# Two hidden layers of a decoder's FFN by seven block products over pairs of token groups

## The reference

```python
x = _layernorm(x + _L0_attn_ref(x, ...))           # a scan over 128 positions, 8 heads
x = _layernorm(x + _L0_xattn_ref(x, ctx, itok, proj_in, proj_out))   # 8 experts, all of them dense
x = _layernorm(x + _L0_ffn_ref(x, ...))

# the FFN: w1, w2 [1024, 256], h1, h2 [1024, 1024], w3 [256, 1024], all ternary (times 8), s: a scale per output
h = silu(x @ w1.T * w1_s) * (x @ w2.T * w2_s)
h = gelu(h @ h1.T * h1_s)
h = gelu(h @ h2.T * h2_s)
return h @ w3.T * w3_s
```

## Time and profile before

| | us |
|---|---|
| median of three runs (784.78 to 785.19) | 784.87 |
| span of the profiled execution, first to last instruction | 783.9 |
| TensorE busy in it | 775.0 (99%) |
| VectorE busy | 485.2 (62%) |
| ScalarE busy | 358.2 (46%) |
| GpSimd busy | 197.4 (25%) |

### The profile page before, as it was taken

The page is one execution under the profiler, slowest core; times in us unless marked ns, Lnnn a source line. Parts: engine busy times, 40 slices in busy tenths (PEclk is TensorE's granted clock), DMA queues, the critical chain, the costliest instruction groups (busy, mean ns, idle before and its releaser), DMA issues.

```text
span 783.9 us, 12001 instructions
## 1 busy us (share of the span) xinstructions
PE 775.0 (99%) x3827; PEld 654.8 (84%) x3827; DVE 485.2 (62%) x1146; ACT 358.2 (46%) x691; POOL 197.4 (25%) x233
## 2 busy tenths in 40 slices
PE   8999999999999999999999999999999999999996
PEld 6788888888888888888888888888888888888886
DVE  4789889876786878788665654327432654255113
ACT  6778743334433434343433364434443354335332
POOL 2776333325342525243342310000000000000001
PEclk9999999999999999999999999999999999999998
DMA  7800000002212231212211000100010001000000
GB/s 258 293 1 1 1 1 1 1 28 82 71 51 95 54 108 41 94 54 80 67 53 42 7 2 1 27 1 27 0 27 0 27 0 27 0 28 1 0 1 29
DMA packets 22414, 32.96 MB, mean 42 GB/s; under 512 B 8161, under 2 KB 12897, under 8 KB 22113
## 3 DMA queue, kind: packets, MB, share of 16 engines
q1 hardware_dynamic: 22080, 32.14, 13.4%
q10 hardware_dynamic: 288, 0.26, 0.1%
HBM read 28.72 MB, written 2.10 MB: 39 GB/s over the span
## 4 chain that ended last, share of the span: by engine, by line
PE 98%; DMA 1%; issue 0%; POOL 0%; ACT 0%; SPq 0%; DVE 0%; POOLq 0%
PE bank L1178 30%; PE bank L1071 15%; PE bank L927 10%; PE bank L955 8%; PE bank L1049 7%; PE bank L1050 7%; PE bank L1054 7%; PE bank L1070 6%; PE bank L1193 4%; PE bank L1074 2%; DMA wp_lo_f<-in_wproj 1%; PE bank L995 0%; PE bank L1027 0%; PE bank L1026 0%; POOL rstd L568 0%
## 5 line engine op out<-in xcount | busy, mean ns | idle before, releaser
L1071 PE MATMUL bank<-wx_both,hx_hi 128*128 128x512 f32 x512 | 191.5, 397 | 0.0
L798 ACT ACTIVATE hx_hi<-bank 128x512 fp32r<-128x512 f32 x128 | 76.4, 597 | 204.9 <-PE bank L1054 203.7
L573 POOL TENSOR_TENSOR x_tok<-right,x_tok 128x256 f32<-128x256 f32 x128 | 95.9, 750 | 210.9 <-ACT right L805 210.9
L1433 DVE SCALAR_TENSOR_TENSOR hx_lo<-bank,hx_hi 128x512 fp32r<-128x512 f32 x128 | 88.2, 689 | 70.9 <-ACT hx_hi L798 69.8
L1071 PEld LDWEIGHTS bank<-wx_both,hx_hi 128*128 128x128 f32 x512 | 96.2, 188 | 16.6
L1070 PE MATMUL bank<-wx_both,hx_lo 128*128 128x256 f32 x384 | 108.8, 283 | 0.0
L1178 PE MATMUL bank<-ha_hi_r,wf_hi_r 128*128 128x512 f32 x256 | 100.1, 391 | 0.0
L1551 DVE TENSOR_TENSOR ha_lo<-hf,ha_hi_r 128x512 fp32r<-128x512 f32 x64 | 44.1, 688 | 90.4 <-ACT hf L892 89.9
L1178 PE MATMUL bank<-ha_lo,wf_hi_r 128*128 128x512 f32 x256 | 99.8, 390 | 0.0
L1178 PE MATMUL bank<-hb_lo,wf_hi_r 128*128 128x512 f32 x256 | 99.7, 390 | 0.0
L1178 PE MATMUL bank<-hb_hi_r,wf_hi_r 128*128 128x512 f32 x256 | 99.7, 389 | 0.0
(11 more groups left out here) (192 smaller groups left out, 1446.9 us busy)
## 6 DMA issues: line engine op xcount, KB each, us to landing
stage<-in_wffn SPq DMA_DIRECT2D x44, 256.0 KB, 2.7
wx_raw<-in_wx SPq DMA_DIRECT2D x16, 512.0 KB, 4.0
x_tok<-in_x SPq DMA_DIRECT2D x1, 2048.0 KB, 12.9
out<-x_tok SPq DMA_DIRECT2D x16, 128.0 KB, 1.8
xs_lo_f<-in_xT SPq DMA_DIRECT2D x3, 512.0 KB, 6.3
wp_lo_f<-in_wproj SPq DMA_DIRECT2D x2, 512.0 KB, 7.3
ctx_sb<-in_ctx SPq DMA_DIRECT2D x1, 1024.0 KB, 6.6
itok_sb<-in_itok SPq DMA_DIRECT2D x1, 1024.0 KB, 8.6
```

Of the source, the lines that this page charges most:

```text
L573: pool.tensor_tensor(row, right[:, j % 2], row, ALU.add).then_inc(s_row_ok, 1)
L798: act.activation(hx_hi[:, place, c], bank[b][:, :], ACT.Relu).then_inc(s_relu_ok, 1)
L1071: mm = pe.matmul(DBANK[j][:, :].rearrange("p (h d) -> p h d", h=2), hx_hi[:, place, c, a], wo_hl[:, :, c], start=(c == 0), stop=(c == XC - 1))
L1433: dve.scalar_tensor_tensor(out=hx_lo[:, place, c], in0=bank[b][:, :], scalar=0.0, in1=hx_hi[:, place, c].bitcast(F32), op0=ALU.max, op1=AL ...
```

## The change

H1 and H2 are computed for two groups at once. The 1024 x 1024 weight is cut into 2 x 2 blocks of 512 x 512 and the activations of a pair of groups into 2 x 2 blocks of 512 features x 512 tokens (f11, f21 of the first group, f12, f22 of the second). Eight block products become seven by a form of Strassen's scheme: three sums of activation blocks per layer (t1 = f12 - f11, t2 = f22 - t1, t4 = f21 - t2 on VectorE; t3 = f22 - f12 on POOL, in place), four sums of weight blocks, and additions of the results (ScalarE copies a bank out, `snap`; VectorE adds the other bank, `block_11`, `block_22`, `block_12`). The gelu then runs once, on the finished block (`curved`). A product is four outputs m x four k x two parts, 32 matmuls.

The weights' block sums are made beside experts 2 to 5: SyncE loads a quad (four blocks of 128 x 512), POOL makes four sums (`block_sum`), ScalarE rounds the seven blocks (`round_checked`), VectorE compares each with its rounded copy (`compare`), SyncE stores them to HBM (`h_dram`, 14 products of 1 MB). In the FFN SyncE loads the product four ahead into a ring of four (`load_product`). W1, W2 and W3 stay in SBUF and come in 12 pieces beside experts 6 and 7. The moving operands' high parts stand in a ring of three tiles. The FFN is written out for two pairs instead of four groups; the normalisation of the inputs of groups 1, 2 and 3 falls into pair 0, that of pair 0's outputs into layer 0 of pair 1, and that of pair 1's outputs behind W3, the second group first. The diff, cut to its core:

```diff
+        CHECKS = [("block", 0), ("block", 2), ("block", 3), ("sum", 0), ("sum", 1), ("sum", 2), ("sum", 3)]
+        MOVING = ["f11", "f21", "t2", "t1", "f12", "f22", "t4"]
+        OF_W3 = ["f12", "f22", "f11", "f21"]
...
@@ SyncE @@
+            def load_product(n):
+                if n >= 4:
+                    sp_.wait_ge(s_h_mm, (n - 3) * KH)
+                layer, i = divmod(n % (2 * PRODUCTS), PRODUCTS)
+                sp_.dma_start(wring[n % 4][:, :, :].bitcast(F32), h_dram[layer, i]).then_inc(wring_in[n % 4], 16)
+                    if not last:
+                        n = (p - 1) * 4 + u // 2
+                        if u % 2 == 0:
+                            if n + 1 < QUADS:
+                                load_quad(n + 1)
+                            store_blocks(n)
+                        else:
+                            store_sums(n)
...
@@ POOL @@
             def pair(p, last):
+                        if u % 2 == 0 and not last:
+                            block_sum((p - 1) * 4 + u // 2, j)
...
+            def third(q, layer):
+                for k in range(KH):
+                    pool.wait_ge(s_h_sum, summed(q, layer, "t1", k))
+                    if layer == 0:
+                        pool.wait_ge(s_f_hf, (q * 2 + 1) * FC + KH + k + 1 + 4)
+                    else:
+                        pool.wait_ge(s_h_act, q * 2 * 16 + 8 + k + 1)
+                    pool.tensor_tensor(part[at_["f12"]][:, k], part[at_["f22"]][:, k], part[at_["f12"]][:, k], ALU.subtract).then_inc(s_h_t3, 1)
...
@@ ScalarE @@
             def pair(p, last):
+                        if not last and c < (3 if u % 2 == 0 else 4):
+                            round_checked(p, u, c if u % 2 == 0 else 3 + c)
...
@@ ScalarE, ffn(q) @@
+                for layer in range(2):
+                    i0 = layer * PRODUCTS
+                    for m in range(KH):
+                        high(q, i0 + 2, m)
+                        snap(q, layer, 0, m)
+                    for m in range(KH):
+                        high(q, i0 + 3, m)
+                        curved(q, layer, "f11", m)
+                    for m in range(KH):
+                        high(q, i0 + 4, m)
+                        snap(q, layer, 2, m)
+                    if q == 0:
+                        keep((2 + layer) * J)
+                    for m in range(KH):
+                        high(q, i0 + 5, m)
+                        snap(q, layer, 3, m)
+                    for m in range(KH):
+                        high(q, i0 + 6, m)
+                        curved(q, layer, "f22", m)
+                    for m in range(KH):
+                        if layer == 0:
+                            high(q, i0 + 7, m)
+                        curved(q, layer, "f12", m)
...
@@ TensorE, ffn(q) @@
+                for layer in range(2):
+                    for i in range(PRODUCTS):
+                        pe.wait_ge(wring_in[n % 4], 16 * (n // 4) + 16)
+                        for m in range(KH):
+                            into = (B1 if i in (1, 3, 5) else A1)[m]
...
+                            elif i == 5:
+                                pe.wait_ge(s_h_add, (q * 2 + layer) * 3 * KH + 4 + m + 1)
+                            for k in range(KH):
+                                if m == 0:
+                                    pe.wait_ge(s_h_lo, tile_n * KH + k + 1)
+                                w = wring[n % 4][:, k, m * P:m * P + P]
+                                pe.matmul(into[:, :], w, b_hi[:, k], start=(k == 0 and i in (0, 1, 3)), stop=False, skip_group_check=True)
+                                mm = pe.matmul(into[:, :], w, b_lo[:, k], start=False, stop=(k == KH - 1), skip_group_check=True)
+                            mm.then_inc(s_h_mm, 1)
...
@@ VectorE, experts @@
+                            if c == 0 and u % 2 == 0 and t > 0 and (not last or u == 0):
+                                compare(t - 1)
+                            if c > 0 and not last:
+                                compare(t + (0 if u % 2 == 0 else 3) + c - 1)
...
@@ VectorE, ahead of the FFN @@
+                norm2_apply(J, 1)
+                norm2_halves(1)
...
@@ VectorE, ffn(q), after the gating product of step n @@
+                        if not first and m < KH:
+                            first_sum(q, 0, m)
+                            low_part(q, 0, m)
+                        elif not first:
+                            second_sum(q, 0, m - KH)
+                            fourth_sum(q, 0, m - KH)
+                            low_part(q, 1, m - KH)
+                    for layer in range(2):
+                        for m in range(KH):
+                            low_part(q, i0 + 2, m)
+                        if q == 0:
+                            norm2_stats(g * J)
+                        elif layer == 0:
+                            row_set(0)
+                        for m in range(KH):
+                            low_part(q, i0 + 3, m)
+                            block_11(q, layer, m)
+                        if q == 0:
+                            norm2_apply(g * J, g)
+                            norm2_halves(g)
+                        elif layer == 0:
+                            y_normed(0, range(J), 1)
+                            row_set(1)
+                        for m in range(KH):
+                            low_part(q, i0 + 4, m)
...
+                        if q == 0:
+                            norm2_words(g)
+                        for m in range(KH):
+                            low_part(q, i0 + 6, m)
+                            block_22(q, layer, m)
+                        def behind(m):
+                            if layer == 0:
+                                first_sum(q, 1, m)
+                                low_part(q, i0 + 7, m)
+                                second_sum(q, 1, m)
+                            else:
+                                low_part(q, i0 + 7, m)
+                        for m in range(KH):
+                            block_12(q, layer, m)
+                            if m > 0:
+                                behind(m - 1)
+                        behind(KH - 1)
+                        if q == 0:
+                            x_low(g)
+                        for m in range(KH):
+                            if layer == 0:
+                                fourth_sum(q, 1, m)
+                            low_part(q, i0 + 8, m)
...
@@ VectorE, the end of pair 1 @@
+                    else:
+                        row_set(2)
+                        y_normed(2, range(J), 3)
+                        y_scaled(3, 0)
+                        y_added(0)
```

More of the change, by code:

```diff
@@ L467, in _, with load_quad @@
             load_expert(0, 2, 7)
-            def pair(p, last):
-                for u in range(8):
-                    if not last or u < 6:
+            def load_quad(n):
+                layer, k = quad(n)
+                if n >= 2:
+                    sp_.wait_ge(s_sum, 4 * (n - 1))
+                    sp_.wait_ge(s_sum_cmp, PRODUCTS * (n - 2) + 3 + 2)
+                    sp_.wait_ge(blocks_out[n % 2], 48 * (n // 2))
+                for half in range(2):
+                    c0 = H_AT[layer] + (half * KH + k) * F
+                    sp_.dma_start(raw_quads[:, n % 2, 2 * half:2 * half + 2].rearrange("p h m -> p (h m)"), wffn[:, c0:c0 + F]).then_inc(stage_in[n % 2], 16)
@@ L480, in pair @@
                         load_expert(0, p * 2 + 2, p * 8 + 4)
-            pairs_of_experts(sp_, pair)
+                    if u == 1 and last:
+                        for i in range(2):
+                            sp_.wait_ge(blocks_out[i], 48 * QUADS // 2)
+                        for n in range(3):
+                            load_product(n)
             sp_.wait_ge(s_up_mm, E * G * XC)
-            sp_.dma_start(s3_b[:, :], w3_s.partition_broadcast(P)).then_inc(s_s3_in, 16)
+            sp_.dma_start(s3_b[:, :], w3_s.partition_broadcast(P)).then_inc(s_small_in, 16)
@@ L484, in _, with turn_halves @@
+            sp_.wait_ge(s_wide_c, 1)
+            load_product(3)
             sp_.wait_ge(s_wide_f, 1)
             wide = sp_.value_load(wide_flag[0:1, 0:1], min_val=0, max_val=1)
[L487 to L492, removed]
+            def turn_halves(g):
                 for j in range(J):
-                    sp_.wait_ge(s_f_halves, g * J + j + 1)
+                    sp_.wait_ge(s_f_halves, (g - 1) * J + j + 1)
@@ L628, in ffn, with ffn_wide @@
+            def ffn_wide(g, first, last):
+                if not first and not last:
                     ln_rstd(s_f_ve, s_f_rstd, g + 2)
                 if last:
[L631 to L635, removed]
@@ L640, in _ @@
             with pool.If(wide < 1):
-                groups(pool, ffn, True)
+                for q in range(PAIRS):
+                    ffn(q)
                 pool.nop()
             with pool.Else():
-                groups(pool, ffn, False)
```

(14 more changed lines are left out.)

630 lines of the change are left out of this document (491 added, 139 removed).

## The result

The median of four runs is **773.63 us** (772.94 to 773.85), beside 785.03 us (784.78 to 785.31) of the kernel before on the same chip: a ratio of 0.9853 (95% interval 0.9842 to 0.9865), 11.4 us less. The forecast was 779.8 us in a range of 763 to 790. So the sign came as forecast, and the gain is more than twice as large. The profiled execution took 772.94 us with a span of 771.0, 12.9 less than the span of before. That is 1.5 more than the medians differ by, since this execution was the shortest of its four and the profiled one of before longer than others: where later runs list both, before has a span of 783.0 to a time of 784.76. So 1.8 us lie around the span, where the prediction read 1.0; the forecast stays, since it is the median of the runs less 5.1.

What follows compares the result with a forecast made beforehand. TensorE, busy 99% of the span, was taken as the bound. Terms -29.1 + 7.8 + 4.4 + 6.6 + 2.5 + 2.2 + 0.5 = -5.1 us gave 779.8 us from a median of 784.87, range 763 to 790.

Steps and rivals of the forecast that it cites:

- The matmuls taken out and their price: H1 and H2 in the FFN: 128 fewer matmuls at 0.2273 us each, -29.1 us.
- the FFN's start: Group 1's normalisation moved ahead of group 0's gating products makes PE wait for the last low part: 2.5 us, once.
- the end: After W3's start, the last group's scalings, additions and statistics queue behind the previous group's normalisations: 2.2 us (1 to 3).
- product 1's gaps: From W1/W2 to the first products, PE waits for DVE's fourth low part, held by `third`: 3.9 us a pair, 7.8 in both.
- product 5: Inside each layer of pair 0, block 22's rounds begin late and product 5 waits: 2.2 us a layer, 4.4 (0 to 6).
- layer 0 to layer 1: At the layer change PE waits for DVE's fourth low part: 3.0 us a pair, plus 0.6 in pair 0, 6.6 in all.
- E: Rival: a granted clock under 1 in the FFN, 6.9 us at the four big stalls; chance 0.10.
- Experts: Added POOL, ACT and DVE work beside the experts costs PE 0.5 us in all (0 to 10).
- Rival C: Exclusive time of POOL and DVE beside the experts makes it slower: four blocks cost 9.6 us, 789 us; chance 0.17.
- D: Rival: the eighth is not saved, waits and ring weights make matmuls dearer, +0.022 us each, 800 us; chance 0.04.
- A: The forecast itself, as a case: 772 to 786 us; chance 0.48.
- B: Rival: POOL and DVE pass each other or hand-overs hide, without both `third` terms 766 us, ends 758 and 772; chance 0.21.

Runs made afterwards that it cites:

- first experiment: Against the changed kernel, GpSimd's third difference waits in both layers until the low parts of the layer's second product are done: 765.41 us, ratio 0.9756.
- fourth experiment: Against the changed kernel, ScalarE's copies and VectorE's low parts of the next group's x moved behind those of the next layer's second product: 773.37 us, ratio 0.9853.
- second experiment: Against the changed kernel, ten matmuls with overwritten result added where TensorE waits for product 1's fourth low part, both pairs: 773.77 us, ratio 0.9853.
- sixth: Against the changed kernel, GpSimd makes two of each four block sums once more into unused memory beside the experts: 774.11 us, ratio 0.9862.
- seventh experiment: Against the changed kernel, the last group's first two scalings, an addition and statistics go ahead of the previous group's four normalisations: 773.46 us, ratio 0.985.

## Why the prediction was right and wrong

**Right.** The matmuls taken out and their price; the FFN's start (2.2 for 2.5); the end (2.2); the place and releaser of product 1's gaps, and that `third` and VectorE's subtractions hold each other. The round from m = 4 on was 3.77 us for 3.98, since `second_sum` got in ahead of `third` and `third` had to wait (1.8 us). In VectorE's and GpSimd's timelines after:

```profile
494.34 0.74 DVE L2103 SCALAR_TENSOR_TENSOR part_f<-bank,scales,silu 128x512 f32<-128x512 f32 x1
495.18 0.69 DVE L2024 TENSOR_TENSOR part_f<-part_f 128x512 f32<-128x512 f32 x1
495.91 1.64 DVE L2031 TENSOR_TENSOR part_f<-part_f 128x512 f32<-128x512 f32 x1
...
495.22 1.77 POOL L807 TENSOR_TENSOR part_f<-part_f 128x512 f32<-128x512 f32 x1 [1.96 <-DVE part_f L2103]
```

That is most of what made the gaps 2.75 us and not 3.9. The Trainium skill ("SBUF — State Buffer", Who interferes with whom) says that a VectorE instruction with two SBUF inputs contends with a GpSimd instruction that reads SBUF, and that the first to issue makes the other wait; the rows agree, in both directions.

**Wrong: product 5, 4.4 us.** The walk put the start of block 22's rounds 9.2 us before product 5's end in pair 0. In the trace of layer 0 they start at 522.95, and product 5 ends at 534.67 (product 6's last matmul at 541.71, less its 31 distances): 11.7 us. VectorE's fourth low part of product 1 (the first of each five below) and the low part that opens block 22's rounds, in layer 0 and in layer 1 of pair 0:

```profile
497.47 3.09 DVE L2012 TENSOR_TENSOR part_r<-part_f,hring 128x512 fp32r<-128x512 f32 x5
...
522.95 0.68 DVE L2012 TENSOR_TENSOR part_r<-part_f,hring 128x512 fp32r<-128x512 f32 x1
...
552.33 3.09 DVE L2012 TENSOR_TENSOR part_r<-part_f,hring 128x512 fp32r<-128x512 f32 x5
...
577.81 0.69 DVE L2012 TENSOR_TENSOR part_r<-part_f,hring 128x512 fp32r<-128x512 f32 x1
```

From the one to the other VectorE takes 25.5 us in both layers; the walk has 26.5 (from 25.2 less 0.69 to 31.1 and four products of 7.27, less 9.2). Of this 1.0 us, 0.4 are block 11's four rounds at 2.6 and not 2.7 us; the rest was not traced. In layer 0 the other 1.5 us are TensorE's: from the end of product 1's stall (498.20) to product 5's end it takes 36.5 us and not 35.0, because of the half clock, and VectorE's chain does not wait for it there. In layer 1 no half clock comes ahead of product 5; the earlier start and the shorter rounds leave 0.75 of the 2.2 us. That the rounds can hold product 5 back was right: with TensorE earlier in the first experiment it waits 2.3 us. That this is so near 2.2 is chance, since there the stall at product 1 is gone.

**Wrong: layer 0 to layer 1, 6.6 us.** The rounds themselves came as walked, 3.5, 3.5 and 2.9 us in pair 1 (`first_sum` at 686.27, 689.79, 693.29, 696.19). The origin failed: "t1 starts 0.05 after product 5's end". It started 2.0 before that end (688.3), because block 22 was done 4 us before it and not 1.85: 1.47 by the half clock, the other 0.7 by VectorE's eight rounds before, 2.6 and not 2.7 us each. So 3.0 became 0.7. In pair 0 the lead was 0.7 us, and 2.0 us of wait are left, named after ScalarE's copies; the fourth experiment shows VectorE's chain just as late.

**The step that failed in both** is the lead of VectorE's rounds over TensorE, which was walked too small. The prediction carries product 1's stall on ("PE then starts product 2 at 31.1") and counts the layer change from product 5's end, but behind the stall it lets TensorE run at full clock: the half clock stands in "Sum" at nothing. It took 1.55 and 1.47 us in the two pairs. I put it to a rival (E, chance 0.10, 6.9 us at the four big stalls), as a pure loss. It came at two of the four, cost 3.0 us there, and gave most of that back as a lead at product 5 and the layer change: this the second experiment shows (2.0 of 2.7 us). The other part of the step is the size of VectorE's chain, walked 0.1 us too long a round, and in pair 0 1.0 us in all up to block 22.

**Experts.** Rival C fell: no stall in any stretch, and six sums for four change nothing in TensorE. The 0.74 us row addition was priced as exclusive, though the earlier trace rows had shown that an instruction with an input in PSUM keeps its time. D fell: the distance is 0.227 wherever TensorE doesn't wait and the clock is 1.00. By time the result lies at the low end of A (772 to 786), just above B's upper end of 772, but B's reason doesn't hold: the engines do collide where I let them, and the gap behind it is there.

## What to carry to other kernels

When one engine sets the end and another chases it, walk both on one clock from the first stall to the last, and carry on all that makes the first one late, the lower clock behind a wait too. Lateness is a cost where it arises and a lead for the chaser at the next place: of 2.7 us saved at product 1, 2.0 came back as later waits. Before a wait is put to one releaser, look for the second chain that ends within the same microsecond; moving the copies of x alone gained nothing here. And where a two-engine loop hands over at every step, put the next step's copy ahead of this step's work in the queue: it took the rounds from 2.6 us to the bound's own step, and took away the wait as the layer changes without removing the hold.

## What the runs showed of the hardware

**The clock after a gap.** Behind the gap of 2.4 to 2.6 us ahead of product 1 the granted clock fell to 0.50 for about 3 us in all twelve cases (six kernels, both pairs), at once or up to some 1.4 us after TensorE had begun again. Behind the 1.9 us gap at the FFN's start it fell in four of eight profiles, though the code up to there is the same for TensorE. Gaps of 0.4 to 1.6 us at the layer change, and one of 2.27 us in the filled kernel, were followed by 1.00. So the length of a gap alone did not decide it, and what did is open. The Trainium skill ("TensorE: Matmul & The Clock Gate", Part 1) has idleness bring the array back to half rate; the rows agree for the gaps of 2.4 us and more, for the one of 1.9 us in half of the profiles, and not for the others. The fall at the FFN's start cost 1.6 us in the filled kernel's profile, by the distances of the matmuls behind the gap; no run was made to price it alone. That is more than the medians of the second, fourth, sixth and seventh experiment differ from the changed kernel's.

**The hold is mutual.** In the first experiment four of GpSimd's subtractions, one right behind the other, met VectorE's low parts of product 2: GpSimd's took 1.68 to 1.74 us each for 1.29 alone, and the three low parts that started beside them 1.77 to 1.79 us each for 0.69 alone.
